# Attention and experts on one core: the preparation with tokens on partitions

## The reference

```python
xn = _layernorm(x, axis=-1)
# attention
q = (x @ Wq.T).reshape(B, S, H, Dh)      # the same for k and v; x is xn here
q, k = _rope(q, k)                       # q * cos + rotate_half(q) * sin
scores = jnp.einsum('bqhd,bkhd->bhqk', q, k) * scale    # causal mask, softmax
out = jnp.einsum('bhqk,bkhd->bqhd', attn, v).reshape(B, S, H * Dh)
return out @ Wo.T
# experts
logits = jnp.einsum('tc,ec->te', x_flat, router_w)      # softmax, top 2, normalised shares
h = jax.nn.relu(jnp.einsum('tc,efc->tef', x_flat, w1) + b1[None])
y = jnp.einsum('tef,ecf->tec', h, w2) + b2[None]
x = x + attention(xn) + experts(xn)
```

## Time and profile before

| | |
|---|---|
| median of 3 runs | 724.39 us (722.64 to 725.66) |
| profiled execution, span | 727.7 us |
| PE, DVE, ACT, POOL busy | 687.2, 575.7, 443.8, 261.2 us |
| preparation until routing begins on DVE | 78.28 us |
| first scores of unit 0 | 105.50 us |
| mean granted clock of PE | 0.974 |

### The profile page before, as it was taken

One profiled execution on the slowest core, in us unless ns is written; L12 is line 12 of the kernel. 1 busy time (PEld: TensorE's weight loads), 2 busy tenths in 40 slices (PEclk: granted clock), 3 DMA queues, 4 the chain that ended last, 5 costly groups with the idle time before them and its releaser, 6 DMA issues.

```text
span 727.7 us, 18476 instructions
## 1 busy us (share of the span) xinstructions
PE 687.2 (94%) x6054; PEld 395.3 (54%) x6054; DVE 575.7 (79%) x1338; ACT 443.8 (61%) x962; POOL 261.2 (36%) x308
## 2 busy tenths in 40 slices
PE   8799898999999999999999999999999999999996
PEld 3456433434444444444999999974444443444543
DVE  6956758998898898998666666668989989999624
ACT  3354115665776766767666766647767677567470
POOL 2565401205546556563000000004444444454641
PEclk9899979989999999999999999999999999999998
DMA  8499952052662751551422222253515426018034
GB/s 233 117 239 242 228 120 31 4 97 56 120 118 67 149 117 41 90 89 42 112 68 69 69 69 69 68 132 59 79 37 84 67 42 99 21 44 198 24 87 118
DMA packets 64622, 69.36 MB, mean 95 GB/s; under 512 B 9935, under 2 KB 52431, under 8 KB 64491
## 3 DMA queue, kind: packets, MB, share of 16 engines
q1 hardware_dynamic: 60394, 60.07, 37.9%
q0 software_dynamic: 4096, 8.40, 4.5%
q10 hardware_dynamic: 64, 0.02, 0.0%
HBM read 41.11 MB, written 26.67 MB: 93 GB/s over the span
## 4 chain that ended last, share of the span: by engine, by line
PE 27%; DVE 19%; issue 5%; DMA 1%; ACT 1%; SPq 1%; ACTq 0%; DVEq 0%
DVE mx L889 9%; PE bank L1410 8%; PE bank L1428 8%; DVE q_high L881 5%; PE bank L1361 3%; PE bank L1326 2%; PE bank L1454 1%; PE bank L1300 1%; PE bank L1419 1%; DVE xn_all L1028 1%; PE bank L1292 1%; DVE xnT L994 1%; PE bank L1468 1%; DVE mx L881 1%; DMA early<-heads_d 1%
## 5 line engine op out<-in xcount | busy, mean ns | idle before, releaser
L764 ACT ACTIVATE probs<-bank 128x512 f32<-128x512 f32 (+2 forms) x640 | 313.6, 555 | 180.1 <-PE bank L1326 159.9
L889 DVE TENSOR_REDUCE mx<-bank 128x2 f32<-128x1024 f32 (+2 forms) x200 | 219.7, 1129 | 44.2 <-PE bank L1300 34.1
L666 POOL TENSOR_SCALAR_AFFINE_SELECT probs<-probs 128x512 f32<-128x512 f32 x128 | 87.4, 684 | 318.0 <-ACT probs L764 313.8
L1326 PE MATMUL bank<-stack 64*128 64x512 f32 (+3 forms) x768 | 188.6, 426 | 8.6 <-ACT probs L764 6.8
L1361 PE MATMUL bank<-probs,vst 128*32 128x256 f32 (+2 forms) x2560 | 192.0, 374 | 2.5 <-POOL probs L666 1.5
L1326 PEld LDWEIGHTS bank<-stack 64*128 64x128 f32 x768 | 87.1, 185 | 130.6 <-ACT probs L764 72.6
L1292 PE MATMUL bank<-stack 64*128 64x512 f32 (+3 forms) x768 | 148.2, 383 | 4.4 <-DVE mx L881 2.5
L881 DVE CUSTOM_DVE_ANT_0 q_high<-bank,later_s 128x384 bf16<-128x384 f32 (+1 forms) x240 | 134.4, 618 | 3.1 <-PE bank L1292 2.6
L1292 PEld LDWEIGHTS bank<-stack 64*128 64x128 f32 x768 | 74.8, 189 | 44.2 <-issue 16.3
L1361 PEld LDWEIGHTS bank<-probs,vst 128*32 128x32 f32 x2560 | 51.4, 108 | 81.0 <-issue 60.1
L649 POOL DMA_INDIRECT k_high<-slots_out_d,slot x64 | 61.6, 962 | 55.3 <-ACT probs L764 50.2
(11 more groups left out here) (138 smaller groups left out, 471.6 us busy)
## 6 DMA issues: line engine op xcount, KB each, us to landing
stack<-parts_d SPq DMA_DIRECT2D x96, 128.0 KB
slots_in_d<-const_s SPq DMA_DIRECT2D x4, 1152.0 KB, 10.2
tiles_s<-slots_in_d SPq DMA_DIRECT2D x72, 64.0 KB, 1.8
slots_out_d<-k_high SPq DMA_DIRECT2D x72, 64.0 KB, 1.6
early<-in_w_experts SPq DMA_DIRECT2D x8, 514.0 KB
stack<-parts_d SPq DMA_DIRECT2D x64, 64.0 KB
parts_d<-probs SPq DMA_DIRECT2D x8, 512.0 KB, 6.1
heads_d<-xnT SPq DMA_DIRECT2D x124, 18.0 KB
```

The source lines that it names most:

```text
L666: pool.affine_select(out=t, in_=t, compare_op=ALU.is_ge, fill=0.0, base=0, pattern=[[0, HG], [1, P]], channel_multiplier=-1).then_inc(s["d ...
L764: nc.scalar.activation(to, src, ACT.Exp, scale=SCALE).then_inc(s["probs_made"], 1)
L889: v.tensor_reduce(to, src.rearrange("p g (a k) -> p g a k", k=w), AX_X, ALU.max, negate=True).then_inc(s["scores_read"], 1)
L1326: made = mm(st_of(u, n, i)[:, col:col + HALF - q0], kstk[r][g][:, hp, kb * P:(kb + 1) * P], qstk[r][g][:, hp, c * HALF + q0:(c + 1) * HALF ...
```

## The change

- Weights: `w_in` holds, for each channel, the columns of q, k, v and the router, 392 in all (`IN`), with q's and k's columns in an order by unit, half, depth and pair of heads; `w_out` holds the output weights. The swapped copies `qs` and `ks` are gone.
- Tokens on partitions: `project_rows(b, i)` makes, for two tiles of 128 tokens, a product of 392 columns each, with the normalised tile as the weights. `products(b, i)` on DVE multiplies q and k of both tiles by the cosines and, reading the other half of each head by address, by the sines; the tables are now 128 columns each and part of the constants. POOL adds (`add_products`). PE transposes the rows back to channels on partitions (`turn_roped`), ACT copies the high part out of PSUM (`keep_high`) and DVE subtracts for the low one (`keep_low`). The low parts lie in stack 3 in the meantime.
- `normalise` moves from DVE to ACT as a scale and a shift; values and logits are copied in four groups per sequence (`keep_values`), each after DVE's products of the group.
- The preparation takes its PSUM in turn from three pairs of banks (`prep_uses`), the early items use the fourth pair alone (`ms_of`). Ten items instead of eleven are made early (`PREPARED`).
- POOL clears the stacks instead of ACT, three in the preparation and the fourth after all parts are written; its ones and its load are issued in unit 0.
- The parts in DRAM are ordered so that a row has both heads of a half, 8 KB. `load_stacks` needs six transfers of rows instead of ten; each repeats its source twice by a leading dimension of stride zero.
- `zero_slots` moves from the preparation to unit 0: two quarters before `store_heads(0, 0)` and two after the maxima rows of unit 1.
- The order of all uses of the maxima's banks is now a list, from which waits and banks are taken; the order within the units is as before.

```diff
+        by_cos = [early[:, NT * C:NT * C + 2 * S], spare[0]]
+        roped_rows = [early[:, NT * C + 2 * S:NT * C + 4 * S], spare[1]]
+        high = [qk_high[:, 0:2 * S], spare[2]]
+        low = [stacks[3][:].rearrange("p a h s -> p (a h s)").bitcast(F32)[:, i * 2 * S:(i + 1) * 2 * S] for i in range(2)]
...
+        PREPARED = {(2, "g2"): 1, (2, "g3"): 1, (3, "r0"): 1, (3, "g0"): 1, (3, "r1"): 1, (3, "g1"): 1, (3, "g2"): 1,
+                    (3, "g3"): 1, (4, "r0"): 1, (4, "r1"): 1}
+
+        prep_uses = [("x", 0, 0), ("g", 0, 0), ("g", 0, 1), ("g", 0, 2), ("x", 1, 0), ("g", 0, 3)]
+        for b in range(1, B):
+            prep_uses += [("r", b - 1, 0), ("g", b, 0), ("r", b - 1, 1), ("g", b, 1)]
+            prep_uses += [("x", b + 1, 0)] * (b + 1 < B) + [("g", b, 2), ("g", b, 3)]
+        prep_uses += [("r", B - 1, 0), ("r", B - 1, 1)]
+
+        def prep_pair(kind, b, i):
+
+            return pair[prep_uses.index((kind, b, i)) % 3]
...
+        def ms_of(use):
+
+            return ms[1] if use < EARLY else ms[(use - EARLY) % 2]
+
+        def read_before(use):
+
+            return use if use < EARLY else use - 1
...
             def keep_parts(b):
 
-                for first, n, part, tile in (("q_first", 0, 0, high_q[b % 2]), ("k_first", 1, 0, high_k[b % 2]),
-                                             ("q_split", 0, 1, rope_q[b % 2]), ("k_split", 1, 1, rope_k[b % 2])):
-                    sp.wait_ge(s[first], b + 1)
-                    sp.dma_start(parts_d[n, b * G:(b + 1) * G, :, part, :, :].rearrange("g h d s -> (g h) d s"), tile
-                                 ).then_inc(parts_written[n][b % 2], 16)
+                for part, made in enumerate(("high_made", "low_made")):
+                    sp.wait_ge(s[made], 2 * b + 2)
+                    for n in range(2):
+                        tile = (high, low)[part][b % 2][:, n * S:(n + 1) * S]
+                        sp.dma_start(parts_d[n, b * G:(b + 1) * G, :, part, :, :, :].rearrange("u g d h s -> (u g) (d h) s"),
+                                     tile).then_inc(parts_written[n][b % 2], 16)
...
                 def rows(n, g, at, part, count):
-                    src = parts_d[n, bass.ds(u, 1), :, part:part + count, :, :].rearrange(
-                        "o (h g) a d s -> g (o a d) h s", g=2)[g]
-                    sp.dma_start((qstk, kstk)[n][r][g][at * DH:(at + count) * DH, :, :].bitcast(F32), src
-                                 ).then_inc(stack_loaded[r], 16)
+
+                    src = parts_d[n, bass.ds(u, 1), g, part:part + count, :, :, :].rearrange("o a d h s -> (o a d) (h s)")
+                    sp.dma_start((qstk, kstk)[n][r][g][at * DH:(at + PARTS * count) * DH, :, :].bitcast(F32).rearrange(
+                        "n h s -> n (h s)"), src.unsqueeze(0).broadcast_to([PARTS, count * DH, PAIRS * S])
+                        ).then_inc(stack_loaded[r], 16)
 
                 for g in range(2):
                     rows(1, g, 0, 0, 2)
-                    rows(0, g, 0, 0, 2)
-                    rows(0, g, 2, 0, 2)
-                    rows(1, g, 2, 1, 1)
-                    rows(1, g, 3, 0, 1)
+                    for part in range(2):
+                        rows(0, g, 2 * part, part, 1)
...
                     if past(u):
                         sp.wait_ge(s["scoresT_made"], banks_before(u, 0))
+                    else:
+                        load_ones(3)
                     load_stacks(u + 3, (r + 3) % 4)
                 if isinstance(u, int) and u == 2:
                     sp.wait_ge(s["b2_zeroed"], 1)
@@ -441,10 +468,16 @@
                     sp.wait_ge(heads_stored[1], 64 * LAST)
                     for b in range(B - 1):
                         load_sums(b)
+                if u == 0:
+                    for i in range(2):
+                        zero_slots(i)
                 store_heads(u, 0)
                 load_expert(u, 0)
                 if more(u, 1):
                     store_max_rows(u + 1, (r + 1) % 4)
+                if u == 0:
+                    for i in range(2, 4):
+                        zero_slots(i)
...
@@ -584,19 +614,17 @@
             pool.memset(eps_s[:], EPS).then_inc(s["eps_ready"], 1)
             pool.memset(ones_b[:], 1.0).then_inc(s["ones_ready"], 1)
 
...
+            def add_products(b, c):
+
+                pool.wait_ge(s["products_made"], 4 * b + 2 * c + 2)
+                cols = slice(c * S, (c + 1) * S)
+                pool.tensor_tensor(roped_rows[b % 2][:, cols], roped_rows[b % 2][:, cols], by_cos[b % 2][:, cols], ALU.add
+                                   ).then_inc(s["roped"], 1)
+
+            def clear_stack(i):
+
+                pool.memset(stacks[i][:].rearrange("p a h s -> p (a h s)").bitcast(F32), 0.0
+                            ).then_inc(s["stack_cleared"], 1)
 
             pool.memset(mrow[0][:], 0.0).then_inc(s["rows_zero"], 1)
             pool.wait_ge(s["rows_zero"], 1)
@@ -617,15 +645,19 @@
             k.done(pool.tensor_copy(masks_b[:], masks_s))
             k.settle()
             pool.sem_inc(s["consts_ready"], 1)
+            for i in range(2):
+                clear_stack(i)
             for b in range(B):
-                split(b)
+                for c in range(2):
+                    add_products(b, c)
+                if b == 0:
+                    clear_stack(2)
...
-            pool.wait_ge(s["v_copied"], B)
+            pool.wait_ge(s["v_copied"], 4 * B)
+            for written in parts_written:
+                for i in range(2):
+                    pool.wait_ge(written[i], 16 * PARTS * 2)
+            clear_stack(3)
...
+            def normalise(b):
+
+                act.wait_ge(s["ln_shift"], b + 1)
+                for t in range(b * T, (b + 1) * T):
+                    last = nc.scalar.activation(xn_all[:, t, :], x_all[:, t, :], ACT.Identity, bias=shift[:, t:t + 1],
+                                                scale=rstd[:, t:t + 1])
+                last.then_inc(s["xn_ready"], 1)
...
+            def keep_values(b, i):
+
+                act.wait_ge(s["products_made"], 4 * b + i + 1)
+                src = prep_pair("g", b, i).rearrange("p (t w) -> p t w", w=HALF)
+                ts = slice(i * CHUNK, (i + 1) * CHUNK)
+                nc.scalar.copy(v_all[:, b * G:(b + 1) * G, ts, :].rearrange("p g t e -> p t g e"),
+                               src[:, :, 2 * C:3 * C].rearrange("p t (g e) -> p t g e", g=G))
+                nc.scalar.copy(logits[:, b * T + i * CHUNK:b * T + (i + 1) * CHUNK, :], src[:, :, 3 * C:IN]
+                               ).then_inc(s["v_copied"], 1)
...
+            def keep_high(b, c):
+
                 if b >= 2:
-                    act.wait_ge(s["logits_made"], b - 1)
-                nc.scalar.copy(xnTs[b % 2], place_of(b, "turned")).then_inc(s["xnT_ready"], 1)
-
-            def keep_logits(b):
-                act.wait_ge(s["logits_made"], b + 1)
-                nc.scalar.copy(logits[:, b * T:(b + 1) * T, :],
-                               place_of(b, "logits")[:, 0:T * E].rearrange("p (t e) -> p t e", e=E)
-                               ).then_inc(s["logits_copied"], 1)
...
+            def products(b, i):
+
+                if b == 1:
+                    dve.wait_ge(s["consts_ready"], 1)
+                dve.wait_ge(s["qkv_made"], 4 * b + i + 1)
+                ts = slice(i * CHUNK, (i + 1) * CHUNK)
+                ps = prep_pair("g", b, i).rearrange("p (t w) -> p t w", w=HALF)[:, :, 0:2 * C]
+                a, r = (t[b % 2].rearrange("p (t w) -> p t w", w=2 * C)[:, ts, :] for t in (by_cos, roped_rows))
+
+                def wide(t):
+                    return t[:, ts, :].unsqueeze(2).broadcast_to([P, CHUNK, 2 * H // PAIRS, t.shape[2]])
+
+                a, r, ps = (x.rearrange("p t (h r) -> p t h r", r=DH * PAIRS) for x in (a, r, ps))
+                v.tensor_tensor(a, ps, wide(cos_s), ALU.mult)
+                d = DH // 2 * PAIRS
+                v.tensor_tensor(r[:, :, :, 0:d], ps[:, :, :, d:2 * d], wide(sin_s[:, :, 0:d]), ALU.mult)
+                v.tensor_tensor(r[:, :, :, d:2 * d], ps[:, :, :, 0:d], wide(sin_s[:, :, d:2 * d]), ALU.mult
+                                ).then_inc(s["products_made"], 1)
+
+            def keep_low(b, c):
+
                 if b >= 2:
-                    dve.wait_ge(s["roped"], 2 * (b - 2) + n)
-                v.tensor_tensor(t[b % 2], ps, cos_s, ALU.mult).then_inc(s[used], 1)
-
-            def sine(b, made, used, written, ps, r):
-
-                dve.wait_ge(s[made], b + 1)
-                if b >= 2:
-                    dve.wait_ge(written[b % 2], 16 * PARTS)
-                v.tensor_tensor(r[b % 2], ps, sin_s, ALU.mult).then_inc(s[used], 1)
-
-            def cos_q(b):
-                cosine(b, "q_made", "q_used", place_of(b, "q"), turned_q, 1)
-
-            def sin_q(b):
...
+            def project_rows(b, i):
+
+                for t in range(i * CHUNK, (i + 1) * CHUNK):
```

(57 more changed lines are left out.)

446 lines of the change are left out of this document (214 added, 232 removed).

## The result

The changed kernel takes **848.09 us** (845.81 to 850.71, 4 runs) where the kernel before takes 724.06 beside it: a ratio of 1.171, 95% interval 1.168 to 1.175. The forecast was 809 in a range of 716 to 900, and slower with 0.77. The profiled execution has a span of 849.0.

A forecast was written before the change was run, and what follows sets the result against it. The prediction took stack loads on 2 of 16 DMA engines to decide: 727.7 + 20.5 ahead of the first scores + 64 in the units = 812, less the profiled run's 3.3 above the median, 809; range 716 to 900.

The forecast's parts named there:

- The mechanism: Stack loads: a leading stride-zero repetition of 2 keeps row transfers on 2 of 16 DMA engines, share near 0.12.
- The price of a load: Stack load on two engines: 512 KB each at 25.5 GB/s, 20.6 us, plus 1.1 for gaps, 21.7 us.
- The rivals with 31 us and with 65: Stack loads: rows in series, 31 us a load, total 948, chance 0.12; or crawling at 65 or more, over 1,000, 0.06.
- The schedule of the compute side: Preparation: low parts at 29.0, first score item to routing 26.8 us, compute ready at 112, covered by the loads.
- no instruction of the slowed kind: DVE in preparation: 10.1 us a sequence, 0.5 of it small scale and shift, with no slowed instruction left.
- Rival 1: Stack loads spread over 16 engines as now: stack 0 at 46, routing at 72.8, 720 us; chance 0.16.
- Ahead of the first scores, +20.5: Preparation: stores and loads in turn on two engines end at 121.3, first scores at 126 instead of 105.5.
- Written, that is 34.0: Preparation: sequence 0's low parts, standing at 29.0, are written at 34.0; load 0 starts 1.5 later.
- 3 for the maxima rows: End of preparation: 3 us for the maxima rows before unit 0's first scores.
- In the units, +64: Units: a load's 26.7 us against 22.4 to the first score stalls PE, adding 64 us in all.
- 8 x 4.3 + 4 x 7.3: Units: eight PE stalls of 4.3 us, four of 7.3 in units 1 to 4, where expert halves come in.

The follow-up runs named there:

- split_rows: Changed kernel with each repeated transfer of stack rows issued as two transfers without the leading repetition of 2, 14 to a stack instead of 8: 734.7 us.
- q_repeat_ahead: `repeat_inside` with the repetition in the rows of q ahead of the 8 rows again instead of behind them: 744.8 us.
- repeat_inside: Changed kernel with a row's two parts side by side in DRAM, k's rows two plain transfers, q's repetition behind the 8 rows: 723.3 us.
- spread_stores: Changed kernel with the part ahead of the units in DRAM, so stores have 128 rows outermost; loads stay on a leading 2: 824.4 us.
- both_spread: `split_rows` with the part ahead of the units in DRAM, stores with 128 rows outermost, every 8 rows loaded by their own transfer: 756.9 us.

## Why the prediction was right, and where its sizes were off

**The mechanism** held: row transfers on 2 of 16 engines. Share 0.13 was foretold as 0.12; `split_rows` changes beside that only the number of transfers, and `q_repeat_ahead` nothing of the bytes, rows or transfers of `repeat_inside`. The Trainium skill's rule (DMA: Bandwidth & Descriptors, Rules for kernel authors) on a leading zero-stride broadcast is borne out, by 53 GB/s in the load and by the 21 us of `q_repeat_ahead`.

**The price of a load**, 21.7 us: the first one took 23.9 from issue to the item behind it, against 23.2 in the forecast (34.0 to 57.2). 25.5 GB/s an engine was taken, 26.5 measured. The rivals with 31 us and with 65 fell.

**The schedule of the compute side** was near: low parts at 30.87 (29.0), a group on DVE 1.32 us (1.26), eight scalings 3.19 us (2.8). The estimate by the Trainium skill (ScalarE: Activation LUTs, What ACT_TABLE_LOAD costs) was 3.2, and the trace agrees. The prediction left "no instruction of the slowed kind" on DVE and took 0.5 us for the small ones; that was wrong, one of 8 columns took 2.30 us twice. First score item to routing is 99.54 - 68.95 = 30.6 us (26.8), part of it at half the clock. Rival 1, all transfers spread, was foretold as 720 with first scores near 101; `repeat_inside` shows 723.3 and 100.95. The agreement at the first scores is partly luck: stack 0 and routing were foretold at 46 and 72.8, and the first item came at 48.74 and routing at 75.56; the stretch behind routing was 3 us shorter than in the forecast.

**Ahead of the first scores, +20.5, measured +36.8.** The step that was sized wrong is "Written, that is 34.0", and with it the load's start at 35.5. I had costed the stores as they were, at share 0.85, though their outer dimension had changed too, from 16 to 8: they run on 8 engines, and the load is issued at 45.07. That the same rule bears on every transfer whose shape the change alters, stores included, was there to be read in the diff. The first item came 11.8 us later than 57.2, and from there to the issue of the maxima rows, at 139.48 when the last parts are written, it was 70.5 us instead of 65.6. The "3 for the maxima rows" held (139.48 to 142.26). PE was ready for the first scores at 125.0 and not at 112, but covered, as foretold. With the stores spread, as the forecast took them to be, `spread_stores` has its first scores at 119.80, 6 us ahead of the 126; so the other terms of that sum were somewhat long, and hid a part of this error.

**In the units, +64, measured +84.5.** The step is "8 x 4.3 + 4 x 7.3". The 11 waits behind unit 0's came to 54.2 - 17.3 = 36.9 us, not 63.6: 3.4 each, so the stalls were sized too large; the 3 us more for the expert halves don't show (3.7, 4.6 and 2.5 us in the first waits behind unit 0's). Missing was what follows a stall: PE busy grew by 55.5 us at a clock of 0.88, a term that the sum doesn't have. The two errors partly cancelled, which is luck; the sum was 20 us short. Of the 39 us between forecast and result, 16 are the first step and 20 this one; how the profiled runs stand to their medians is the rest.

**Why it is not the rest of the change.** With the transfers spread, preparation is 4.5 us shorter in the profiled runs (100.95 against 105.50), and nothing of it can be told in the medians (0.999, 0.996 to 1.002). No version measured beats the kernel before by more than the measurement can tell.

## What to carry to other kernels

For every transfer whose shape a change alters, stores too, read the outermost dimension that can't be joined to the next: at 2 this kernel's DMA share was 0.13, at 8 it was 0.5, at 64 rows 0.98. A repetition with stride zero belongs behind the rows, or in two transfers; a smaller number of transfers is not a cheaper load: 8 took 848 us, 14 with the same bytes 735. Then look who stands behind a long load in its queue, and price a wait of PE with what its clock loses behind it: here 37 us of waits in the units came with 55 us of slower matmuls.

## What the runs showed of the hardware

- An engine's rate depends on the shape of the load and not only on its count: 26.5 GB/s with 2 engines and 8 or 16 rows for each (53 GB/s at 0.13), 8 GB/s with 8 engines and one 8 KB row each (66 GB/s at 0.51, `both_spread`), 8 to 13 GB/s an engine in `split_rows`, with transfers of 8 and of 16 rows (86 to 143 GB/s at 0.65 to 0.95). So the spread load is only twice as fast as that on 2 engines, 11.9 against 23.9 us to the first item. What sets this was not tried.
- Issuing is not free: three transfers took SP 12.84 us at 56.59, against 1.94 at 45.07, and a single one of them 9.24. That a full queue is the reason was inferred.
- Reading 2 x 8 rows with an even stride is the same transfer as 16 rows (share 1.11).
- One DVE instruction of 8 columns (the shift of the normalisation) took 2.30 us at 22.78 and 37.57, where an addition of POOL of 2.34 us runs beside it, and 0.17 at 13.99, beside a memset of POOL.
